# Layer-1 self-attention of a two-layer decoder: GpSimd adds the two key tiles' probabilities before TensorE sums them

## The reference

```python
def _L1_attn_ref(x, W_qkv, b_qkv, W_out, b_out):
    HIDDEN = 128
    NUM_HEADS = 16
    HEAD_SIZE = 64
    B, S, _ = x.shape
    qkv = x @ W_qkv + b_qkv
    qkv = qkv.reshape(B, S, 3 * NUM_HEADS, HEAD_SIZE)
    Q = qkv[:, :, :NUM_HEADS, :]
    K = qkv[:, :, NUM_HEADS:2 * NUM_HEADS, :]
    V = qkv[:, :, 2 * NUM_HEADS:, :]
    scores = jnp.einsum('bqhi,bkhi->bhqk', Q, K) / jnp.sqrt(jnp.float32(HEAD_SIZE))
    mask = jnp.triu(jnp.full((S, S), -10000.0, dtype=scores.dtype), k=1)
    scores = scores + mask
    probs = jax.nn.softmax(scores, axis=-1)
    vals = jnp.einsum('bkhi,bhqk->bqhi', V, probs)
    vals = vals.reshape(B, S, NUM_HEADS * HEAD_SIZE)
    return vals @ W_out + b_out
```

## Time and profile before

| what | value |
|---|---|
| time, median of 3 runs (lowest to highest) | 2070.24 us (2063.59 to 2086.78) |
| time of the profiled execution | 2072.13 us |
| span of the profile (first to last instruction) | 2070.3 us |
| TensorE busy | 1744.3 us, 84% |
| VectorE, ScalarE, GpSimd busy | 54%, 43%, 11% |
| mean granted TensorE clock | 0.914 of full speed |

### The profile page before, as it was taken

One profiled execution on the slowest core, in us unless ns is written; L12 is line 12 of the kernel. 1 busy time (PEld: TensorE's weight loads), 2 busy tenths in 40 slices (PEclk: granted clock), 3 DMA queues, 4 the chain that ended last, 5 costly groups with the idle time before them and its releaser, 6 DMA issues.

```text
span 2070.3 us, 49773 instructions
## 1 busy us (share of the span) xinstructions
PE 1744.3 (84%) x20200; PEld 1119.5 (54%) x20216; DVE 1116.0 (54%) x2297; ACT 896.5 (43%) x1641; POOL 235.8 (11%) x392
## 2 busy tenths in 40 slices
PE   3787768777759499799899889989979979988995
PEld 1454434444459456556556655655655655664663
DVE  5565666757664352662572474365366267257344
ACT  2443534434412154453453454444445345345443
POOL 0000100001026300100110010010010010001001
PEclk9876988979969799899999989989989989998997
DMA  7300000000067500000010010010000001000000
GB/s 282 128 21 25 14 20 21 24 14 14 13 143 93 159 17 4 19 25 3 2 42 3 3 41 3 3 39 4 3 19 24 4 3 40 3 3 6 2 2 6
DMA packets 51287, 66.89 MB, mean 32 GB/s; under 512 B 6599, under 2 KB 41905, under 8 KB 50243
## 3 DMA queue, kind: packets, MB, share of 16 engines
q1 hardware_dynamic: 47971, 60.23, 9.0%
q0 software_dynamic: 2560, 3.46, 2.0%
q10 hardware_dynamic: 576, 0.39, 0.1%
HBM read 41.73 MB, written 24.12 MB: 32 GB/s over the span
## 4 chain that ended last, share of the span: by engine, by line
PE 62%; issue 15%; DVE 11%; ACT 7%; POOL 2%; DMA 2%; SPq 0%; ACTq 0%; DVEq 0%; POOLq 0%
PE psum L753 6%; PE psum L665 5%; PE psum L526 5%; DVE peak L1147 5%; PE psum L868 4%; PE psum L718 4%; ACT prob L1024 3%; PE psum L766 3%; PE psum L551 3%; PE psum L539 3%; PE psum L821 2%; PE psum L660 2%; PE psum L583 2%; PE psum L618 2%; PE psum L714 2%
## 5 line engine op out<-in xcount | busy, mean ns | idle before, releaser
L1024 ACT ACTIVATE prob<-psum 128x1024 f32<-128x1024 f32 (+2 forms) x384 | 340.0, 916 | 346.1 <-PE psum L672 185.0
L1147 DVE TENSOR_REDUCE peak<-psum 128x4 bf16<-128x1024 f32 (+2 forms) x304 | 363.8, 1221 | 211.4 <-PE psum L594 132.8
L1317 POOL TENSOR_TENSOR rstd<-moments,eps 128x2 f32<-128x2 f32 x80 | 16.3, 204 | 1380.9 <-DVE moments L1065 1380.9
L526 PE MATMUL psum<-xt,w_late 128*128 128x256 f32 x512 | 136.8, 407 | 14.8 <-issue 9.7
L665 PE MATMUL psum<-qt,kt 64*128 64x256 f32 x1024 | 131.8, 376 | 0.0
L868 PE MATMUL psum<-w_late,qt 128*128 128x128 f32 x1024 | 129.1, 285 | 0.7
L1154 DVE RECIPROCAL rsum<-psum 128x128 f32<-128x128 f32 x32 | 30.6, 956 | 180.7 <-PE psum L766 159.0
L868 PEld LDWEIGHTS psum<-w_late,qt 128*128 128x128 f32 x1024 | 124.0, 200 | 6.5 <-issue 3.2
L753 PE MATMUL psum<-prob,v_big 128*64 128x256 f32 x1024 | 124.6, 385 | 0.0
L618 PE MATMUL psum<-kb,qb 32*128 32x512 bf16 x320 | 73.7, 456 | 50.3 <-DVE peak L1147 19.9
L526 PEld LDWEIGHTS psum<-xt,w_late 128*128 128x128 f32 x512 | 93.1, 196 | 40.2 <-issue 14.9
(11 more groups left out here) (254 smaller groups left out, 3113.7 us busy)
## 6 DMA issues: line engine op xcount, KB each, us to landing
zd<-kx SPq DMA_DIRECT2D x24, 512.0 KB, 5.1
union<-zd SPq DMA_DIRECT2D x16, 768.0 KB, 4.7
xg<-union SPq DMA_DIRECT2D x16, 192.0 KB, 2.0
w_late<-in_w1T SPq DMA_DIRECT2D x1, 2816.0 KB, 12.2
kt<-in_w2T SPq DMA_DIRECT2D x4, 704.0 KB
union<-in_x SPq DMA_DIRECT2D x16, 128.0 KB, 2.2
union<-in_xT SPq DMA_DIRECT2D x16, 128.0 KB, 2.2
xtd<-x_out SPq DMA_DIRECT2D x16, 128.0 KB, 1.9
```

The source lines that it names most:

```text
L526: last = mm(bank[:, j * 256:(j + 1) * 256], w[:, c * 128:(c + 1) * 128], x, start=True, stop=True)
L1024: nc.scalar.activation(prob[s][:, slot + 2 * i:slot + 2 * i + 2, 0:n], v.pair(step, i)[:, :, 0:n], ACT.Exp, scale=a.scale).then_inc(v.free ...
L1147: nc.vector.tensor_reduce(dst, src, axis=AX.X, op=ALU.max).then_inc(v.free(step), 1)
```

## The change

For groups 0, 1 and 2 the sixteen summing matmuls behind P are gone. When TensorE has finished the product of such a group, GpSimd adds key tile 0's probabilities to those of key tile 1 in place, one instruction of 128 x 1024 float32, and a new step **U** `(g)` lets TensorE sum the result with eight matmuls. Group 3 is summed as before, in P. U waits for GpSimd's add. In a stream's list U of group g stands ahead of T of group g + 2 (which overwrites that part of `prob`), U of group 2 behind P of group 3. The bank of sums is now closed by U of group 2. The table of turns has the six new steps in it and is otherwise the same order of steps.

```diff
 def head_steps(a, s):
     out = []
     for g in range(ROUNDS_T[a]):
+        if a is L1 and g > 1:
+            out.append(("U", a, s, g - 2))
         out += [("T", a, s, g, k) for k in range(2 if a is L1 else 1)]
         if g:
             out.append(("P", a, s, g - 1))
-    return out + [("P", a, s, ROUNDS_T[a] - 1)]
+    return out + [("P", a, s, ROUNDS_T[a] - 1)] + ([("U", a, s, 2)] if a is L1 else [])
...
-          "A2 B A D B A B C A B C B C B2 A2 B3 C A B5 A B A B A B2 A4 B5 A2 B2 A3 B A B A5 B2 A2 B2 A4 B4 A B "
...
+          "B A D B A B C A B C B C B2 A2 B3 C A B5 A B A B A B2 A4 B5 A2 B2 A3 B A B A5 B2 A2 B2 A4 B5 A B2 A B "
...
-AHEAD1, AHEAD3 = (36, 31, 0, 0), (43, 46, 4, 4)
+AHEAD1, AHEAD3 = (36, 31, 0, 0), (46, 49, 4, 4)
...
                     last.then_inc(v.full(*o_fill), 1)
-                    if g == 0:
-                        pe.wait_ge(*v.may_fill(*d_fill))
-                    sums = v.bank(*d_fill)
-                    for k in range(2):
-                        for u in range(2):
-                            for t in range(2):
-                                for j in range(2):
-                                    r, c = 64 * t + 32 * j, 256 * j + 128 * t
-                                    last = mm(sums[r:r + 32, 0:128], ones_g[:, u, g, :],
-                                              prob[s][:, slot + 2 * k + u, c:c + 128],
-                                              start=(g == 0 and k == 0 and u == 0),
-                                              stop=(g == 3 and k == 1 and u == 1))
                     if g == 3:
-                        last.then_inc(v.full(*d_fill), 1)
+                        sums = v.bank(*d_fill)
+                        for k in range(2):
+                            for u in range(2):
+                                for t in range(2):
+                                    for j in range(2):
+                                        r, c = 64 * t + 32 * j, 256 * j + 128 * t
+                                        mm(sums[r:r + 32, 0:128], ones_g[:, u, g, :], prob[s][:, slot + 2 * k + u, c:c + 128],
+                                           start=False, stop=False, skip_group_check=True)
...
+            elif kind == "U":
+                g, d_fill = step[3], (("P", a, s, 0), 0)
+                pe.wait_ge(y.tiles_added[s], v.at(3, g + 1))
+                if g == 0:
+                    pe.wait_ge(*v.may_fill(*d_fill))
+                for u in range(2):
+                    for t in range(2):
+                        for j in range(2):
+                            r, c = 64 * t + 32 * j, 256 * j + 128 * t
+                            last = mm(v.bank(*d_fill)[r:r + 32, 0:128], ones_g[:, u, g, :],
+                                      prob[s][:, 4 * (g % 2) + 2 + u, c:c + 128], start=(g == 0 and u == 0),
+                                      stop=(g == 2 and u == 1), skip_group_check=True)
+                if g == 2:
+                    last.then_inc(v.full(*d_fill), 1)
...
+            if kind == "P" and a is L1 and step[3] < 3:
+
+                g = step[3]
+                pool.wait_ge(*v.filled(step, 1 if g == 0 else 0))
+                of = [flat(prob[s][:, 4 * (g % 2) + 2 * k:4 * (g % 2) + 2 * k + 2, :]) for k in range(2)]
+                nc.gpsimd.tensor_tensor(of[1], of[0], of[1], ALU.add).then_inc(y.tiles_added[s], 1)
```

More of the change, by code:

```diff
@@ L117 @@
           "B2 A B D A B A2 B4 A B2 A D A B2 A B2 A2 B2 A")
-TURNS3 = ("A B5 A B A2 B A3 B A2 B2 A B A B A B A2 B2 A B A B A B A B A D B2 A B2 A B A B2 A B A B D A2 B2 D "
-          "A2 B A D B A B C A B C B C B2 A2 B3 C A B5 A B A B A B2 A4 B5 A2 B2 A3 B A B A5 B2 A2 B2 A4 B4 A B "
-          "A B A B A B A B5 A2 B A B2 A3 B A2 B A7 B A3")
-AHEAD1, AHEAD3 = (36, 31, 0, 0), (43, 46, 4, 4)
+TURNS3 = ("A B5 A B A2 B A3 B A2 B2 A B A B A B A2 B2 A B A B A B A B A D B2 A B2 A B A B2 A B A B D A2 B2 D A2 "
+          "B A D B A B C A B C B C B2 A2 B3 C A B5 A B A B A B2 A4 B5 A2 B2 A3 B A B A5 B2 A2 B2 A4 B5 A B2 A B "
+          "A B A B A B6 A2 B A B2 A4 B A3 B A8 B A3")
+AHEAD1, AHEAD3 = (36, 31, 0, 0), (46, 49, 4, 4)
 def interleaved(streams, turns, aheads):
@@ L162, in fills @@
         return ["Q"]
-    if kind in ("D", "L", "C", "CK", "RN", "RL", "Z", "Y") or kind == "W" and step[3]:
+    if kind in ("D", "L", "U", "C", "CK", "RN", "RL", "Z", "Y") or kind == "W" and step[3]:
         return []
@@ L383, in __init__ @@
                     self.routed_in = n("routed_in")
+                    self.tiles_added = n("tiles_added")
         p1, p3 = Sync("p1"), Sync("p3")
```

## The result

| | median | ratio to before, 95% interval |
|---|---|---|
| before, beside these runs | 2075.47 us (4 runs) | |
| changed kernel | 2129.8 us (2093.6 to 2141.8, 4 runs) | 1.027 (1.018 to 1.037) |

The change makes the kernel slower, by 2.7% as the ratio has it. The two runs that were not slow, 2093.60 and 2119.13 us, have a mean 1.5% above the median of before, and the two slow ones, 2140.46 (the profiled one) and 2141.80 us, have one 3.2% above it. So the runs give the sign, and the size rests on the profile and on e5, which repeats the change.

The account below looks back on a forecast made before the run. TensorE was taken to bound the layer-1 self-attention rounds. Net waiting of +4.65 us a pass, +37 us in eight, plus 18 us of clock made +55 us on a 2070 us median: about 2125 us, range 2097 to 2158.

Parts of the forecast that it names:

- The bound: Phase 3's first 89.3 us a pass: TensorE busy 89.13 us, so each microsecond of its work or waiting counts fully.
- A2: Stream A, group 2: products 2 and 3 share a bank, so the second waits for ScalarE's copy; +0.24 us a pass.
- B0: Stream B, group 0: nothing stands between product and sums; a TensorE stop of 2.4 us, +1.97 us a pass.
- B1: Stream B, group 1: one 0.62 us step of stream A stands between; a stop of 1.7 us, +1.35 us a pass.
- A1: Stream A, group 1: nothing stands between product and sums; a stop of 2.4 us, +1.96 us a pass.
- B2: Stream B, group 2: over 5 us of work covers the add; 0.51 us gained less 0.15 us waiting, -0.36 us.
- A0: Stream A, group 0: both output projections, 3.8 us, cover the add; -0.51 us a pass.
- The clock: TensorE's clock halving behind one and a half of three stops a pass: 2.2 us a pass, 18 us in all.
- a clock that stays up: Rival: the three stops a pass leave TensorE's clock alone, time 2107 us; chance 0.20.
- contention: Rival: VectorE's SBUF work stretches GpSimd's add to 3.2 us; 2147 us, or 2165 with every clock loss; chance 0.20.
- waits that are taken in elsewhere: Rival: TensorE's 13.7 us of waiting a pass in the other stretch takes in the stops, so not slower; chance 0.08.
- the full gain: Rival: no stop counts at all, so 24 us are saved, 2046 us; chance 0.04.

Follow-up runs that it names:

- e5: The changed kernel itself, unaltered, run again on another chip beside other runs of the kernel before: ratio 1.025, +59.8 us from first value product to end.
- e1: Changed kernel without GpSimd's add and the wait, the eight matmuls summing key tile 0 alone: ratio 0.982 to before, -17.6 us from first product on.
- e3: Changed kernel with the add on VectorE in place of GpSimd: ratio 1.002 to before, +15.1 us from first product on.
- e8: Changed kernel with two GpSimd adds in a row, written to other buffers, the first unread: one run, ratio 1.084 to before, +197.9 us.
- e7: Kernel before with all sixteen summing matmuls, plus GpSimd's six adds a pass that nobody reads: ratio 0.998 to before, -0.2 us.
- e2: Changed kernel with throwaway TensorE matmuls ahead of the three exposed waits: ratio 1.021 to before, +41.2 us from first product on.
- e6: Changed kernel with throwaway TensorE matmuls ahead of the three exposed waits, repeated on another chip: ratio 1.014 to before, +39.6 us.

## Why the prediction was right

The forecast was 2125 us, the median 2129.8; with runs from 2094 to 2142 us so close a hit is chance, and what bears the forecast out is the profile, +57.7 us and in e5 +59.8 us where it had +55. Point by point:

- **The bound** held: in this stretch each microsecond of TensorE's waiting was one of the pass (e1, e3, e8), and what GpSimd did was free where nobody waited (e7).
- **The gain**, 3.06 us a pass by matmuls: came out at 2.6 us. Eight matmuls with their start take 0.58 us (1301.25 to 1301.83), not half of sixteen, 0.51, so a group saves 0.44 us. (The 2.85 us less of busy time are another sum: up to A3's product 56 matmuls are gone, as A2's U comes behind it, and busy time counts each drain ahead of a stop.)
- **The add**, 2.3 us from the slope between 2 and 256 columns: 2.35 us. The slope of the slower row, 3.2 us, played no part.
- **The way** from product to sums, 4.35 us: 4.50 at B0 and 4.43 at the other exposed ones. GpSimd started 2.04 us behind the product's start, not 1.99. The way back from GpSimd had been taken as short as ScalarE's 0.04 us; from the add's end to the sums at B0 (from 1467.98, the pass of the half clock) it is 0.12 us:

```profile
1470.02 2.34 POOL L1324 TENSOR_TENSOR prob<-prob 128x1024 f32<-128x1024 f32 x1 [27.00 <-PE psum L756]
...
1472.48 0.65 PE L832 MATMUL psum<-prob,ones_g 128*32 128x128 f32 x16 [2.56 <-POOL prob L1324]
```

- **The places**: stops of 2.4, 1.7 and 2.4 us at B0, B1, A1 were forecast, 2.56, 1.87 and 2.49 came; B2, A0 and A2 covered, as forecast; the wait for the shift 0.15 us, came with 0.16; the wait for the shared bank at A2 put product 3 at 2.62 us behind product 2, came with 2.63.
- **The waiting in sum**: +37 us forecast, 4.65 a pass. Two terms were a little small: 0.07 us in each of six U and 0.08 to 0.15 us in each of three ways, 0.7 us a pass, which would make 43 us. e2 and e6, which have the waiting alone, came to +41.2 and +39.6, some of it the clock behind the rounds, as in e1.
- **The clock**: 18 us forecast with ends at 0 and 36 as the least certain term; 16.5 to 20.2 measured. The price of one fall, 1.5 us from the row at 0.59, was right: 1.55 us. How many of the 24 stops would have one was a guess between rows that disagreed, 12; it was 10 in the change and 12 in e5, so that part is luck. That it would be B1's and A1's stops and never B0's, nothing in the prediction told.

The rivals fell each by its own run: a clock that stays up by e2 and e6 against e5, contention by e7 and by the add's 2346 ns, waits that are taken in elsewhere by e8 and the change itself (nothing of what was taken vanished), the full gain by the stops themselves.

## What to carry to other kernels

Before work is moved to another engine, write down what the bound engine has in its in-order queue between the step that releases the helper and the step that needs it: only that much of the helper's time is free, and the rest is paid in full and perhaps again in clock. If the queue is dense there, buy distance (a buffer of one's own for the result, the consumer one or two steps later) before the change is judged; here it turned +2.7% into -0.9%. And look at what the removed work was covering: the sixteen matmuls had hidden the copy that frees a shared bank.

## What the runs showed of the hardware

In an otherwise full stretch the granted clock of TensorE fell behind stops of 1.87 and 2.49 us, in five of eight passes and in e5 in six, and never behind one of 2.56 us that stood ahead of them, with the same instructions around; each fall cost about 1.55 us. With stops of 0.7 to 1.4 us (e3) it never fell there. Throwaway matmuls in the stops kept it up in every pass, and saved 16 to 20 us though nobody read what they made. Three stops of 4.2 to 4.9 us a pass with two short ones brought the clock of the phase to 0.89 and cost 66 us beside 73 us of added waiting. A GpSimd addition of 128 x 1024 float32 took 2.35 us against 1.22 us on VectorE, and 48 of them beside full TensorE work cost nothing measurable.
